# Two-layer spectral block on one core: the forward W transform folded on half rows (64x32 tiles), the inverse W transform in 64x64 tiles

## The chip, the cores and the metric

One of the eight cores of a Trainium2 chip runs the kernel. The metric is the device time of one execution in microseconds. Three executions of the kernel before gave 526.34 us as the median, 525.83 us as the lowest and 531.92 us as the highest.

## The reference

The input `x` has shape (4, 45, 90, 384): batch, H, W, channels. Two layers follow one another. Each takes a two-dimensional Fourier transform over H and W, keeps the 23 columns kw = 0 to 22 (all 45 rows of kh), mixes the channels in 8 blocks of 48 with two small dense layers, applies a soft threshold, transforms back and adds its input.

```
# layer 0                                       # layer 1
Xh = f.real - f.imag                            xr, xi = real(xs), imag(xs)
o1 = relu(Xk @ w1[0] + b1[0])                   o1r = relu(xr@w1[0] - xi@w1[1] + b1[0])
o2 = o1 @ w2[0] + b2[0]                         o1i = relu(xi@w1[0] + xr@w1[1] + b1[1])
spec = softshrink(o2, 0.01)                     o2r, o2i = softshrink(second dense layer)
y = ifft2(spec).real + x                        y = irfft2(o2r + 1j*o2i) + x
```

The kernel never goes back to the image between the layers. Layer 0's result is added in the frequency domain (only its even part along kh matters for kw = 0), and a single inverse transform at the end is added to `x` and written out.

## The kernel before

The work is split into 8 tasks, one per batch image and half of the channels (`HC` = 192). A task has six steps of four kw each (the last has three), so there are 48 steps (`STEPS`, `NSTEPS`). `schedule()` writes the order of all work by hand, and every engine walks through the same list, executes its own part and waits on semaphores. Each engine's queue is in order.

**Forward W** ("fwd", lines 402 to 408, 468 to 472, 552 to 574). An image lies in SBUF with W on 90 partitions (`img`, three buffers). A group is four rows of H. TensorE multiplies with `w_fwd` (90 of 128 rows, 64 columns) in two 128x64 tiles, each over 384 columns (two rows of H), into one PSUM bank of the pair P3. ScalarE (for task 0 VectorE, L472) copies the bank to `fs`, and SyncE writes it to DRAM scratch `scr_f` with two DMAs (L284). There are 12 groups per task, 23 DMAs. Groups of task t+1 run in steps 1, 2 and 3 of task t: two before A, two behind it.

**The step.** SyncE loads four kw of `scr_f` into `bt` (L297, 3,072 contiguous bytes per partition row). A is forward H (L618), copied by ScalarE and VectorE to `xs`; GpSimd computes re minus im (`xd`, L362). C0 and D0 (L634, L644, 64x64 tiles) are layer 0's dense layers. VectorE forms its soft-thresholded result `nt`, and GpSimd subtracts it from the real part in `xs` (L369). C1 and D1 (L656, L669) are layer 1's dense layers. T (L681) transposes `nt`, VectorE adds it to `ns` (L533), E (L694) is inverse H, copied to `et`, which SyncE writes to `scr_i` (L303).

**Inverse W** ("inv", L605 and L551). SyncE reads rows of `scr_i` into `jr` (L322, L326). A group is four rows of H: two 64x128 tiles, K = 48 of 64 rows, 90 of 128 columns, 384 moving columns each, into both banks of P3. VectorE adds both banks to `img` (90 x 768, L551); GpSimd stores eight rows (L378) and later loads the next image into their place (L354). In the last task the 12 groups use all eight banks, and four of them (`LAST_POOL`) are added by GpSimd behind a ScalarE copy (L456, L386).

The order within a step s is: load(s+2), C1(s-1), inverse, E(s-2), inverse, C0(s), D1(s-1), D0(s), two forward groups, A(s+1), two forward groups, T(s-1), inverse. Three inverse groups per step run in steps 3, 4, 5 and in step 0 of the task after.

```
for r in range(f_dmas(g)):
    a, b = h0 + 2 * r, min(h0 + 2 * r + 2, h1)
    last = mm(ps[64 * r:64 * r + 64, P3 + g % 2, 0:(b - a) * HC], K["w_fwd"],
              img[t % IMGS][:, a:b, :].rearrange("p h c -> p (h c)"), start=True, stop=True)
```

## Time and profile before

| what | us |
|---|---|
| median of three executions | 526.34 |
| the profiled execution, its own time | 527.67 |
| its span, first to last instruction | 525.8 |
| TensorE matmuls busy | 480.0 |
| VectorE busy | 303.9 |
| ScalarE busy | 208.8 |
| GpSimd busy | 172.8 |

The profile comes from one execution; 527.67 us lies 1.33 us above the median, and 1.9 us of it lie outside the span. PE is TensorE's matmuls, PEld its weight loads, DVE VectorE, ACT ScalarE, POOL GpSimd, SPq SyncE's queue of DMA issues. An fp32 matmul shows as two MATMUL records, so the number behind "x" in a row of PE is twice the number of matmuls in the code. In a timeline row the first number is the start, the second the time to the end of the last of the merged instructions; since matmuls overlap at their ends, the path is read from start to start.

### The profile page before, as it was taken

What the parts mean: (1) busy time and instruction counts of PE and PEld (TensorE: products, weight loads), DVE (VectorE), ACT (ScalarE), POOL (GpSimd) and SP (SyncE); (2) the same over time, 40 slices, a digit from 0 to 9 for tenths busy, and PEclk for the clock granted to TensorE, in tenths of its full rate; (3) what the DMA queues carried; (4) which work ended last, traced back from release to release, by engine and by line L of the source; (5) the groups of instructions that cost most, each with busy time, mean ns of one, the idle gap of its engine ahead of it and who ended that gap; (6) DMA issues with size and microseconds to landing.
All of it is one profiled execution on the core that took longest, in us unless ns stands there. A gap on an engine that the chain in (4) does not pass through costs nothing.

```text
span 525.8 us, 14875 instructions
## 1 busy us (share of the span) xinstructions
PE 480.0 (91%) x6144; PEld 347.5 (66%) x6144; DVE 303.9 (58%) x674; ACT 208.8 (40%) x473; POOL 172.8 (33%) x194
## 2 busy tenths in 40 slices
PE   4549999999999999999999999999999999998772
PEld 1137777767777677767777676777777777876531
DVE  6413456456764577456764577456763677566642
ACT  0014544554354433554354433454345433433101
POOL 9703133113432134313442133312442123222124
PEclk9858999999999999999999999999999999999967
DMA  8859955476899588877889688886989565735397
GB/s 187 268 141 218 272 149 150 105 205 181 253 222 244 154 210 246 238 202 184 263 216 236 173 208 242 228 213 176 255 221 248 167 175 156 156 84 141 108 242 223
DMA packets 76720, 104.65 MB, mean 199 GB/s; under 512 B 7761, under 2 KB 63303, under 8 KB 76526
## 3 DMA queue, kind: packets, MB, share of 16 engines
q1 hardware_dynamic: 57622, 55.97, 39.8%
q0 software_dynamic: 10608, 40.45, 29.1%
q10 hardware_dynamic: 8424, 7.28, 5.5%
q8 instruction: 50, 0.82, 0.7%
q14 instruction: 16, 0.13, 0.1%
HBM read 52.23 MB, written 51.43 MB: 197 GB/s over the span
## 4 chain that ended last, share of the span: by engine, by line
PE 79%; DMA 6%; DVE 6%; POOL 3%; ACT 2%; issue 2%; SPq 1%; ACTq 0%; POOLq 0%; DVEq 0%
PE ps L605 13%; PE ps L669 13%; PE ps L694 12%; PE ps L656 11%; PE ps L572 10%; PE ps L618 9%; PE ps L681 5%; PE ps L634 4%; DMA scr_f<-fs 3%; PE ps L644 3%; DVE img L551 2%; DVE ns L525 2%; ACT p L442 1%; POOL img L386 1%; POOL xs L369 1%
## 5 line engine op out<-in xcount | busy, mean ns | idle before, releaser
L551 DVE TENSOR_TENSOR img<-ps,img 90x768 f32<-90x768 f32 x92 | 82.7, 900 | 23.0 <-PE ps L605 18.1
L369 POOL TENSOR_TENSOR xs<-xs,nt 128x360 f32<-128x360 f32 (+1 forms) x48 | 41.5, 865 | 149.3 <-DVE nt L503 121.7
L605 PE MATMUL ps<-jr,cst 64*128 64x384 f32 (+1 forms) x358 | 83.6, 535 | 7.2 <-DVE img L551 5.7
L572 PE MATMUL ps<-img,cst 128*64 128x384 f32 (+1 forms) x368 | 72.2, 506 | 12.4 <-DMA img<-x 7.6
L378 POOL DMA_DIRECT2D y<-img x42 | 34.6, 825 | 136.0 <-DVE img L551 135.6
L618 PEld LDWEIGHTS ps<-cst,bt 128*64 128x64 f32 x1472 | 63.2, 141 | 21.0 <-issue 13.9
L435 ACT ACTIVATE o<-ps,wt 97x180 f32<-97x180 f32 (+1 forms) x96 | 33.8, 405 | 107.2 <-PE ps L656 107.1
L618 PE MATMUL ps<-cst,bt 128*64 128x90 f32 x1472 | 69.0, 248 | 6.7 <-DMA bt<-scr_f 6.7
L525 DVE SCALAR_TENSOR_TENSOR ns<-p,ps 109x384 f32<-109x384 f32 x96 | 53.2, 554 | 37.9 <-ACT p L442 33.0
L669 PE MATMUL ps<-wt,o 128*64 128x96 f32 x1472 | 73.9, 250 | 0.5 <-DVE o L517 0.5
L669 PEld LDWEIGHTS ps<-wt,o 128*64 128x64 f32 x1472 | 64.9, 137 | 12.6 <-issue 12.6
L656 PE MATMUL ps<-xs,wt 64*97 64x180 f32 (+1 forms) x768 | 68.6, 315 | 2.6 <-POOL xs L369 1.8
L694 PE MATMUL ps<-ns,cst 64*90 64x192 f32 x736 | 71.0, 323 | 0.0
L694 PEld LDWEIGHTS ps<-ns,cst 64*90 64x90 f32 x736 | 62.8, 155 | 7.4 <-issue 1.1
L656 PEld LDWEIGHTS ps<-xs,wt 64*97 64x97 f32 x768 | 57.4, 161 | 13.3 <-POOL xs L369 5.7
L442 ACT ACTIVATE p<-ps 109x384 f32<-109x384 f32 x96 | 47.0, 490 | 27.3 <-PE ps L669 27.3
L408 ACT ACTIVATE fs<-ps 112x384 f32<-112x384 f32 x84 | 38.9, 475 | 36.3 <-PE ps L572 27.2
L517 DVE TENSOR_SCALAR o<-ps,wt 97x180 f32<-97x180 f32 (+1 forms) x96 | 33.8, 394 | 33.3 <-PE ps L656 33.3
L572 PEld LDWEIGHTS ps<-img,cst 128*64 128x64 f32 x368 | 24.7, 141 | 40.7 <-issue 35.5
L488 DVE COPY xs<-ps 128x360 f32<-128x360 f32 (+1 forms) x48 | 24.8, 517 | 44.5 <-PE ps L618 44.5
L533 DVE TENSOR_TENSOR ns<-ps,ns 109x192 f32<-109x192 f32 x96 | 29.8, 352 | 33.5 <-PE ps L681 32.7
L605 PEld LDWEIGHTS ps<-jr,cst 64*128 64x128 f32 x358 | 32.1, 192 | 25.6 <-issue 13.0
(41 smaller groups left out, 411.5 us busy)
## 6 DMA issues: line engine op xcount, KB each, us to landing
y<-img POOLq DMA_DIRECT2D x35, 540.0 KB, 5.5
img<-x POOLq DMA_DIRECT2D x30, 540.0 KB, 8.5
scr_i<-et SPq DMA_DIRECT2D x48, 270.0 KB, 5.7
scr_f<-fs SPq DMA_DIRECT2D x176, 72.0 KB, 3.4
bt<-scr_f SPq DMA_DIRECT2D x40, 270.0 KB, 4.6
jr<-scr_i SPq DMA_DIRECT2D x48, 216.0 KB, 5.1
img<-x ACTq DMA_DIRECT2D x10, 540.0 KB, 7.4
y<-img SPq DMA_DIRECT2D x11, 270.0 KB, 3.8
```

The costliest lines, as they stand in the source:

```text
L369: nc.gpsimd.tensor_tensor(re, re, nt[s % 2][:, :, 0:kws(s), 0:H], ALU.subtract).then_inc(re_ok, 1)
L378: pool.dma_start(out[b, r0:r1, :, f * HC:(f + 1) * HC].rearrange("h w c -> w h c"), img[k][0:W, r0:r1, :]).then_inc(y_st[k][c], 16)
L408: nc.scalar.activation(fs[k][0:rows, 0:cols], ps[0:rows, P3 + g % 2, 0:cols], ACT.Copy).then_inc(f_cp, 1)
L442: nc.scalar.activation(p1[0:rows, p, :], ps[0:rows, P2 + p, 0:2 * HC], ACT.Relu).then_inc(d1_p, 1)
L525: nc.vector.scalar_tensor_tensor(out=ns[0:rows, p].rearrange("p n r c -> p (n r c)"), in0=p1[0:rows, p, :], scalar=2 * LAM, in1=ps[0:rows, ...
L551: nc.vector.tensor_tensor(y, p, y, ALU.add).then_inc(i_add, 1)
L572: last = mm(ps[64 * r:64 * r + 64, P3 + g % 2, 0:(b - a) * HC], K["w_fwd"], img[t % IMGS][:, a:b, :].rearrange("p h c -> p (h c)"), start= ...
L605: last = mm(ps[:, B0 + r, 0:n], K["w_inv"][64 * r:64 * r + 64, :], set_rows(t, j)[64 * r:64 * r + 64, at, 0:n], start=True, stop=True)
L618: last = mm(ps[64 * ab:64 * ab + 64, P0 + q, k * 2 * H:(k + 1) * 2 * H], bt[s % BT][:, at:at + 64], K["h_fwd"], start=True, stop=True)
L656: last = mm(ps[0:2 * BS + 1, P2 + ab, q * STEP * H:q * STEP * H + n], w1[k, im, 2 * f + q, :], xt[k, q, 0:kws(s), im * H:(im + 1) * H], st ...
L669: last = mm(ps[64 * r:64 * r + 64, P2 + p, b * 2 * BS:(b + 1) * 2 * BS], o11[:, b, 2 * p + r, :], w21[:, block_no(s // STEPS, b), :], star ...
L694: last = mm(ps[0:2 * H, P0 + r, p * HC:(p + 1) * HC], K[("h_inv_re", "h_inv_im")[im]][k, :], ns[k, p, :, im, :], start=im == 0, stop=im == 1)
```

## The change

Image rows are folded. W = 90 is cut into halves of 45 columns and H = 45 into halves of 23 and 22 rows: partitions 0 to 44 hold the W positions of the first H half, 64 to 108 those of the second, and the two W halves r = 0, 1 lie side by side in the free dimension. A group is now four j (rows of a half), that is eight rows of H; a task has six (`CH`).

- **New step "uv".** Before the forward matmuls VectorE writes u = half 0 + half 1 and GpSimd writes v = half 0 - half 1, each 128 x 768 fp32, both inputs in SBUF, into one of two buffers. u gives the even kw, v the odd ones.
- **Forward W.** Eight matmuls per group, K = 45 of 64 rows, 32 columns, 384 moving columns, in the eight 64x32 tiles of the array, into both banks of P3. ScalarE does both copies for all tasks. SyncE stores a group with eight DMAs of 24 partitions x 1,536 bytes: 48 per task.
- **Scratch layouts.** `scr_f` and `scr_i` have kw outermost and 48 slots of H instead of 45; a load into `bt` has 96 partition rows, each of four runs of 768 bytes.
- **Inverse W.** Still 12 groups per task; a group is now four j of both H halves for one W half: four 64x64 tiles of 384 columns. VectorE's addition has 109 partitions; the groups of the last set take two additions each.
- **Images.** Loads and stores are split by H half: 8 loads and 8 stores per task in four chunks, refills at their own places in the order. The buffers are cleared whole; `img1` is now cleared by VectorE and `img2` by GpSimd behind the forward groups of task 0. SyncE issues half of task 0's image loads.
- `FS` goes from 4 to 3, `JR` from 3 to 4, `LAST_POOL` from (1, 4, 7, 10) to (1, 4, 7, 9).

```diff
-IMGS, FS, BT, JR = 3, 4, 3, 3
-LAST_POOL = (1, 4, 7, 10)
-JSETS = [(0, 3), (3, 6), (6, 9), (9, 11), (11, 12)]
...
+WR, HR = W // 2, -(-H // 2)
+CH = -(-HR // 4)
+ROWS = 64 + WR
+GROUPS = 2 * CH
+CHUNKS = [(0, 2), (2, 4), (4, 5), (5, 6)]
+NXC = len(CHUNKS)
+IMGS, FS, BT, JR = 3, 3, 3, 4
+LAST_POOL = (1, 4, 7, 9)
+
+KWO = list(range(0, KWP, 2)) + list(range(1, KWP, 2))
+SLOTS = [(p, 4 * i + 2 * a + s) for a in range(2) for i in range(CH) for p in range(2) for s in range(2)]
...
+    order = [("uv", 0, 0), ("uv", 0, 1)]
+    for g in range(CH):
+        order.append(("fwd", 0, g))
+        if g + 2 < CH:
+            order.append(("uv", 0, g + 2))
+    order += [("clear", 1), ("clear", 2), ("load", 0), ("load", 1), ("a", 0), ("x", 0), ("x", 1)]
...
-            fwd[s] = [("fwd", t + 1, 4 * (i - 1) + k) for k in range(4)]
+            fwd[s] = [("fwd", t + 1, 2 * (i - 1) + k) for k in range(2)]
...
+        uv = [("uv",) + f[1:] for f in fwd[s]]
+        ahead = [("uv",) + f[1:] for f in fwd[s + 1]] if s + 1 < NSTEPS else []
...
+        order += uv[1:2]
...
-        order += fwd[s][0:2]
+            order.append(("x", 2 * s + 2))
+        order += fwd[s][0:1]
...
+        order += fwd[s][1:2]
...
+        order += ahead[0:1]
...
-        scr_f = [nc.dram_tensor(f"scr_f{t}", (H, 2, KWP, HC), F32, kind="Internal").ap() for t in range(TASKS)]
-        scr_i = [nc.dram_tensor(f"scr_i{t}", (KWP, 2, H, HC), F32, kind="Internal").ap() for t in range(TASKS)]
...
+        scr_f = [nc.dram_tensor(f"scr_f{t}", (KWP, 2, 2, CH, 2, 2, HC), F32, kind="Internal").ap() for t in range(TASKS)]
+        scr_i = [nc.dram_tensor(f"scr_i{t}", (KWP, 2, 2, 4 * CH, HC), F32, kind="Internal").ap() for t in range(TASKS)]
...
+        def x_loaded(t, g):
+            k, used, c = t % IMGS, t // IMGS, chunk_of(g)
+            if t == 0:
+                return x_first[g], 32
+            if t == 1:
+                return x_second[c], 32
+            return x_ld[k][c], 32 * (used + (k == 2))
...
+        def added(t, g):
+
+            before = [m for m in range(g + 1) if t < TASKS - 1 or m not in LAST_POOL]
+            return i_add, t * (GROUPS + 2) + len(before) + len([m for m in before if m // 2 == CH - 1])
...
+            for g in range(CH):
+                j0, j1 = jrange(g, g + 1, 1)
+                sp.wait_ge(x_odd if g % 2 else x_clr[0], g // 2 + 1)
+                sp.dma_start(folded(0, 1, j0, j1), rows_of(x[0], HR + j0, HR + j1, 0)).then_inc(x_first[g], 16)
...
-                    n, (h0, h1) = t * GROUPS + g, hrows(g)
+                    n = t * CH + g
                     k = n % FS
-                    sp.wait_ge(f_cp, n + 1)
-                    for r in range(f_dmas(g)):
-                        a, b = h0 + 2 * r, min(h0 + 2 * r + 2, h1)
-                        sp.dma_start(scr_f[t][a:b].rearrange("h e k c -> (e k) h c"),
-                                     fs[k][64 * r:64 * r + 2 * KWP, 0:(b - a) * HC].rearrange("q (h c) -> q h c", c=HC)).then_inc(f_st[k], 16)
+                    for p in range(2):
+                        sp.wait_ge(f_cp, 2 * n + p + 1)
+                        for a in range(2):
+                            for o in range(2):
+                                sp.dma_start(scr_f[t][o * KWP // 2:(o + 1) * KWP // 2, :, p, g, a].rearrange("k e s c -> (k e) (s c)"),
+                                             fs[k][64 * a + 32 * o:64 * a + 32 * o + KWP, p, :]).then_inc(f_st[k], 16)
...
-                    rows = scr_f[t].rearrange("h e k c -> (h e) k c")[:, STEP * i:STEP * i + kws(s), :]
-                    sp.dma_start(bt[s % BT][0:2 * H, 0:kws(s) * HC].rearrange("p (k c) -> p k c", c=HC), rows).then_inc(b_ld[s % BT], 16)
+                    rows = scr_f[t][STEP * i:STEP * i + kws(s)].rearrange("k e p g a s c -> (e p g a s) k c")
+                    sp.dma_start(bt[s % BT][0:2 * len(SLOTS), 0:kws(s) * HC].rearrange("p (k c) -> p k c", c=HC), rows).then_inc(b_ld[s % BT], 16)
...
+                        m = t * CH + j - JR
+                        sp.wait_ge(i_mm, 2 * (m + 1))
+                    for a in range(2):
+                        sp.dma_start(set_rows(t, j)[64 * a:64 * a + 2 * KWP].rearrange("q p c -> q (p c)"),
+                                     scr_i[t][:, :, a, 4 * j:4 * j + 4, :].rearrange("k e h c -> (k e) (h c)")).then_inc(landed, 16)
...
+                        c, p = divmod(s, 2)
+                        j0, j1 = jrange(*CHUNKS[c], p)
+                        pool.wait_ge(x_clr[2], 1)
+                        pool.dma_start(folded(2, p, j0, j1), rows_of(x[1], HR * p + j0, HR * p + j1, 0)).then_inc(x_ld[2][c], 16)
+                if kind == "clear" and what[0] == 2:
+                    nc.gpsimd.memset(img[2][:], 0.0).then_inc(x_clr[2], 1)
+                if kind == "uv":
                     t, g = what
-                    c, k, (b, f) = g // 2, t % IMGS, divmod(t, HALVES)
-                    r0, r1 = c * XCH, min(c * XCH + XCH, H)
-                    pool.wait_ge(i_add, t * GROUPS + g + 1)
-                    pool.dma_start(out[b, r0:r1, :, f * HC:(f + 1) * HC].rearrange("h w c -> w h c"), img[k][0:W, r0:r1, :]).then_inc(y_st[k][c], 16)
-                    if c > 0:
-                        refill(t, c - 1)
+                    n, (j0, j1) = t * CH + g, jrange(g, g + 1)
+                    pool.wait_ge(*x_loaded(t, g))
+                    if n >= 2:
+                        pool.wait_ge(f_mm, n - 1)
+                    nc.gpsimd.tensor_tensor(uv[n % 2][:, 1, 0:j1 - j0, :], img[t % IMGS][:, j0:j1, 0, :], img[t % IMGS][:, j0:j1, 1, :],
+                                            ALU.subtract).then_inc(v_ok, 1)
...
+                    t, g = what
+                    c, k, (b, f) = chunk_of(g // 2), t % IMGS, divmod(t, HALVES)
+                    pool.wait_ge(*added(t, g))
+                    for p in range(2):
+                        j0, j1 = jrange(*CHUNKS[c], p)
+                        pool.dma_start(rows_of(out[b], HR * p + j0, HR * p + j1, f), folded(k, p, j0, j1)).then_inc(y_st[k][c], 16)
+                if kind == "refill" and what[0] + IMGS < TASKS:
+                    t, c = what
+                    k, (b, f) = t % IMGS, divmod(t + IMGS, HALVES)
+                    pool.wait_ge(y_st[k][c], 32 * (t // IMGS + 1))
+                    for p in range(2):
+                        j0, j1 = jrange(*CHUNKS[c], p)
+                        pool.dma_start(folded(k, p, j0, j1), rows_of(x[b], HR * p + j0, HR * p + j1, f)).then_inc(x_ld[k][c], 16)
...
-                if kind == "fwd" and what[0] > 0:
+                if kind == "fwd":
...
-                    n, (h0, h1) = t * GROUPS + g, hrows(g)
-                    k, rows, cols = n % FS, (112, 2 * KWP)[g == GROUPS - 1], min(2, h1 - h0) * HC
+                    n = t * CH + g
                     if n >= FS:
-                        act.wait_ge(f_st[k], f_stored((n - FS) // GROUPS, (n - FS) % GROUPS))
...
-                    nc.scalar.activation(fs[k][0:rows, 0:cols], ps[0:rows, P3 + g % 2, 0:cols], ACT.Copy).then_inc(f_cp, 1)
+                    for p in range(2):
+                        nc.scalar.activation(fs[n % FS][:, p, :], ps[:, P3 + p, 0:2 * HC], ACT.Copy).then_inc(f_cp, 1)
...
-                if kind == "fwd" and what[0] == 0:
+                if kind == "clear" and what[0] == 1:
+                    nc.vector.memset(img[1][:], 0.0).then_inc(x_clr[1], 1)
+                if kind == "uv":
...
+                    if n >= 2:
+                        dve.wait_ge(f_mm, n - 1)
+                    nc.vector.tensor_tensor(uv[n % 2][:, 0, 0:j1 - j0, :], img[t % IMGS][:, j0:j1, 0, :], img[t % IMGS][:, j0:j1, 1, :],
+                                            ALU.add).then_inc(u_ok, 1)
...
-                    t, g = what
-                    h0, h1 = hrows(g)
...
+                    B0 = P3 if t < TASKS - 1 else 2 * (what[1] % 4)
+                    j0, j1 = jrange(g, g + 1)
+                    dve.wait_ge(i_mm, t * GROUPS + what[1] + 1)
+                    if j1 - j0 == 4:
+                        y = img[t % IMGS][0:ROWS, j0:j1, r, :].rearrange("p (a s) c -> p a s c", a=2)
+                        p = ps[0:ROWS, B0:B0 + 2, 0:2 * HC].rearrange("p a (s c) -> p a s c", s=2)
+                        nc.vector.tensor_tensor(y, p, y, ALU.add).then_inc(i_add, 1)
...
+                        for a in range(2):
+                            y = img[t % IMGS][0:ROWS, j0 + 2 * a:min(j0 + 2 * a + 2, j1), r, :]
+                            p = ps[0:ROWS, B0 + a, 0:(2, 1)[a] * HC].rearrange("p (s c) -> p s c", c=HC)
+                            nc.vector.tensor_tensor(y, p, y, ALU.add).then_inc(i_add, 1)
...
-                    for r in range(f_dmas(g)):
-                        a, b = h0 + 2 * r, min(h0 + 2 * r + 2, h1)
-                        last = mm(ps[64 * r:64 * r + 64, P3 + g % 2, 0:(b - a) * HC], K["w_fwd"],
-                                  img[t % IMGS][:, a:b, :].rearrange("p h c -> p (h c)"), start=True, stop=True)
+                    n = t * CH + g
+                    pe.wait_ge(u_ok, n + 1)
+                    pe.wait_ge(v_ok, n + 1)
+                    vacate(0)
+                    vacate(1)
+                    for a in range(2):
+                        for o in range(2):
+                            for p in range(2):
+                                q, m = 64 * p, 64 * a + 32 * o
+                                last = mm(ps[m:m + 32, P3 + p, 0:2 * HC], w_fwd[q:q + 64, o, :],
+                                          uv[n % 2][q:q + 64, o, 2 * a:2 * a + 2, :].rearrange("w s c -> w (s c)"), start=True, stop=True)
                     last.then_inc(f_mm, 1)
-                    tenant[g % 2] = [(f_cp, t * GROUPS + g + 1)]
+                    for p in range(2):
+                        tenant[p] = [(f_cp, 2 * n + p + 1)]
...
-                    for r in range((h1 - h0 + 1) // 2):
-                        n = min(2, h1 - h0 - 2 * r) * HC
-                        last = mm(ps[:, B0 + r, 0:n], K["w_inv"][64 * r:64 * r + 64, :], set_rows(t, j)[64 * r:64 * r + 64, at, 0:n], start=True, stop=True)
+                            pe.wait_ge(*last_added(what[1] - 4))
+                    for p in range(2):
+                        for a in range(2):
+                            m, c = (min(2, HR - 4 * g - 2 * a)) * HC, slice(64 * a, 64 * a + 64)
+                            last = mm(ps[64 * p:64 * p + 64, B0 + a, 0:m], w_inv[c, r, :], set_rows(t, g)[c, p, 0:m], start=True, stop=True)
                     last.then_inc(i_mm, 1)
-                    tenant[0] = tenant[1] = [(i_add, t * GROUPS + g + 1)]
```

## Rows read from the trace of the kernel before

**Rows 1.** The page's first two parts: busy time by engine, span in 40 slices.
```profile
PE 480.0 (91%) x6144; PEld 347.5 (66%) x6144; DVE 303.9 (58%) x674; ACT 208.8 (40%) x473; POOL 172.8 (33%) x194
...
PE   4549999999999999999999999999999999998772
...
PEclk9858999999999999999999999999999999999967
```

**Rows 2.** The page's chain that ended last, by engine.
```profile
PE 79%; DMA 6%; DVE 6%; POOL 3%; ACT 2%; issue 2%; SPq 1%; ACTq 0%; POOLq 0%; DVEq 0%
```

**Rows 3.** TensorE's timeline, steps without inverse: start us, duration us, what.
```profile
207.38 1.46 PE L618 MATMUL ps<-cst,bt 128*64 128x90 f32 x32
208.88 0.66 PE L681 MATMUL ps<-cst,nt 128*109 128x128 f32 x4
...
215.18 1.51 PE L572 MATMUL ps<-img,cst 128*64 128x384 f32 x8
216.52 1.41 PE L618 MATMUL ps<-cst,bt 128*64 128x90 f32 x32
217.76 1.46 PE L572 MATMUL ps<-img,cst 128*64 128x384 f32 x8
219.15 0.69 PE L681 MATMUL ps<-cst,nt 128*109 128x128 f32 x4
...
221.09 1.46 PE L694 MATMUL ps<-ns,cst 64*90 64x192 f32 x16
222.48 0.54 PE L634 MATMUL ps<-xd,wt 64*64 64x180 f32 x8
```

**Rows 4.** The same timeline, a step with inverse groups.
```profile
230.80 0.81 PE L605 MATMUL ps<-jr,cst 64*128 64x384 f32 x4
231.44 1.47 PE L694 MATMUL ps<-ns,cst 64*90 64x192 f32 x16
232.75 0.92 PE L605 MATMUL ps<-jr,cst 64*128 64x384 f32 x4
233.60 0.54 PE L634 MATMUL ps<-xd,wt 64*64 64x180 f32 x8
234.07 1.54 PE L669 MATMUL ps<-wt,o 128*64 128x96 f32 x32
235.54 0.54 PE L644 MATMUL ps<-o,wt 64*64 64x180 f32 x8
```

**Rows 5.** All engines' timeline of the start: GpSimd's clears, SyncE's stores of task 0.
```profile
9.02 14.65 POOL L344 MEMSET img<- 64x8640 f32 x2
...
9.86 16.63 SPq L284 DMA_DIRECT2D scr_f<-fs  x23
```

**Rows 6.** The chain of waits at the start: the first A.
```profile
31.16 2.69 PE ps L618 x32
```

**Rows 7.** SyncE's queue in steady state, two steps with forward groups.
```profile
222.26 1.98 SPq L284 DMA_DIRECT2D scr_f<-fs  x4
...
226.38 4.72 SPq L284 DMA_DIRECT2D scr_f<-fs  x8
```

**Rows 8.** Groups of instructions, shapes apart: busy us, mean ns, idle before.
```profile
L551 DVE TENSOR_TENSOR img<-ps,img 90x768 f32<-90x768 f32 x84 | 79.9, 953 | 21.7 <-PE ps L605 16.9
...
L408 ACT ACTIVATE fs<-ps 112x384 f32<-112x384 f32 x77 | 37.5, 490 | 36.3 <-PE ps L572 27.2 <-DMA scr_f<-fs 9.0
...
L386 POOL TENSOR_TENSOR img<-p,img 90x768 f32<-90x768 f32 x4 | 7.3, 1818 | 5.8 <-ACT p L456 5.8
```

**Rows 9.** DMA issues: count, KB each, median us to landing.
```profile
scr_i<-et SPq DMA_DIRECT2D x48, 270.0 KB, 5.7
...
bt<-scr_f SPq DMA_DIRECT2D x40, 270.0 KB, 4.6
```

**Rows 10.** VectorE's timeline in the step of rows 4.
```profile
233.87 0.94 DVE L551 TENSOR_TENSOR img<-ps,img 90x768 f32<-90x768 f32 x1
234.73 0.39 DVE L492 TENSOR_SCALAR o<-ps,wt 128x180 f32<-128x180 f32 x1
```

More of the change, by code:

```diff
@@ L103, in schedule @@
 def schedule():
-    order = [("fwd", 0, g) for g in range(GROUPS)]
-    order += [("load", 0), ("load", 1), ("a", 0), ("x", 0)]
+    order = [("uv", 0, 0), ("uv", 0, 1)]
[4 more added lines that the diff above has]
+    order += [("clear", 1), ("clear", 2), ("load", 0), ("load", 1), ("a", 0), ("x", 0), ("x", 1)]
     fwd, inv = [[] for _ in range(NSTEPS + 2)], [[] for _ in range(NSTEPS + 2)]
@@ L141, in schedule @@
             order += [("rows", t - 1, j) for j in range(JR)]
-        order += fwd[s][2:4]
-        if s < 2:
-            order.append(("x", 2 * s + 2))
+        if i == 1 and t > 1:
+            order.append(("refill", t - 2, 2))
+        order += fwd[s][1:2]
+        if s < 3:
+            order.append(("x", 2 * s + 3))
         if 0 < s <= NSTEPS:
@@ L147, in schedule @@
         order += inv[s][2:3]
+        order += ahead[0:1]
+        if i == 1 and t > 1:
+            order.append(("refill", t - 2, 3))
     order += held
-    order += [("rows", TASKS - 1, j) for j in range(len(JSETS))]
+    order += [("rows", TASKS - 1, j) for j in range(CH)]
     order += [("inv", TASKS - 1, g) for g in range(GROUPS)]
@@ L265, in last_added @@
                 return i_pool, LAST_POOL.index(g) + 1
-            return i_add, (TASKS - 1) * GROUPS + len([m for m in range(g + 1) if m not in LAST_POOL])
+            return added(TASKS - 1, g)
         def block_no(t, n):
@@ new lines, in _ @@
+                if kind == "inv" and what[0] < TASKS - 1 and (what[1] + 1) // 2 in [b for a, b in CHUNKS] and what[1] % 2 == 1:
+                    t, g = what
[4 more added lines that the diff above has]
+                        pool.dma_start(rows_of(out[b], HR * p + j0, HR * p + j1, f), folded(k, p, j0, j1)).then_inc(y_st[k][c], 16)
```

229 lines of the change are left out of this document (96 added, 133 removed).

## The prediction

> **What bounds the kernel now.** I read the page's busy times first: TensorE's matmuls take 480.0 of 525.8 us, no other engine more than 304, and from the fourth slice to the thirty-sixth TensorE is at 9 tenths or more [rows 1]. The chain that ended last says the same by another road: 79% of it is TensorE, SyncE's issues 1%, DMA 6% [rows 2]. So between about 40 and 475 us time is TensorE's start-to-start time, step by step, and I take it from its timeline. The start and the tail are different: in the first three slices TensorE is at 4 to 5 tenths, and the first A begins at 31.16 us [rows 6]. There the order is loads, forward W, stores, load, A, and nothing covers it. A change that makes TensorE cheaper and the road to the first A longer gains in one place and loses in the other.
>
> **Forward W on TensorE, -15.7 us.** Today a step with forward groups spends 1.34 us on the first two groups, 1.24 on A between them, 1.39 on the other two: 3.97 us [rows 3]. An inverse group is two waves of 384 columns in two tiles and takes 0.64 us to the next start [rows 4]: 0.32 us a wave. C0, two waves of 180 columns in four tiles, takes 0.47 us [rows 4]; at 0.15 a wave that leaves 0.17 for changing tile shape on both sides. A takes 1.50 us between operations of other shapes and 1.24 between forward groups of its own shape [rows 3]. The new group is 16 records in eight tiles: two waves if all eight run side by side, so 2 x 0.32 + 0.17 = 0.81 us. Then the step costs 0.81 + 1.50 + 0.81 = 3.12, 0.85 less. 21 steps (7 tasks) give 17.9; today's 12th group streams a quarter of the others' columns, which I count as 0.3 us a task, 2.2 in all, so 15.7. No row shows four column tiles. The bound above is that only four tiles run at once, as in C0: four waves, 1.45 us a group, 4.40 a step, which is 0.43 x 21 + 2.2 = 11.2 us more than today. I take eight, because the four of C0 did run as four. The Trainium skill, "TensorEngine Tiling (Array Packing)", section "Available Configurations", lists 64x32 as eight independent tiles; that would be the same 0.81.
>
> **Inverse W on TensorE, +7 us.** The waves don't change: two waves of 384. What changes is the neighbour. The first group of a step now sits between C1 and E, all in 64-row, 128-column tiles, and costs 0.64 [rows 4]. In 64x64 tiles it costs 0.81, and C1 and E each pay part of a change, 0.06 to 0.1 (E takes 1.39 before C0 without an inverse group between and 1.31 before one [rows 3, 4]): +0.3. The second, between E and C0 (0.85 today), now has C0's shape: -0.15. The third, behind T, pays again before C1: +0.1. Net +0.25 for three; 26 such sets of three give +7. Ends: 0 if the drain hides, +12 if each change costs the 0.17 in full and more.
>
> **The start, +12 us.** SyncE issues 23 stores from 9.86 us in 16.63 us, the last at about 26.5, and A starts 4.7 us later [rows 5, 6]. It will issue 48. GpSimd has done its first clears at 9.02 us [rows 5]; v takes 1.8 (as 90 x 768 in L386), the first group 1.5 (0.81 at a clock that falls as low as 5 tenths in the first three slices [rows 1]), ScalarE's two copies 1.0 [rows 8], so the first store leaves at 13.5. In steady state SyncE issues one per 0.50 us (4 in 1.98) to 0.59 (8 in 4.72) [rows 7]. I take 0.50: 24 us, last store at 37.5, 11 later than now. `bt` loads are cut from 3,072-byte to 768-byte runs, like `scr_i`'s stores of the same size, 5.7 us against 4.6 [rows 9]: +1.1. A starts at 43.3. Low end: if small DMAs went out as fast as v and u allow (6 x (1.8 + 0.95) = 16.6 us), +5; high end 0.59 each, +16. The clears of `img1` (VectorE) and `img2` (GpSimd) take 7.3 us each if both go like GpSimd's two in 14.65 [rows 5]. They lie beside the stores; without that cover they would add up to 7.
>
> **VectorE and ScalarE in the steps, +7 us.** u costs 0.95 us if it goes like the inverse addition of the same 768 elements [rows 8]; one is queued between E's copy and the second inverse addition. In a step with inverse groups today the addition runs from 233.87 to 234.81 and C0's relu from 234.73 to 235.12; D0, which needs it, starts at 235.54 [rows 4, 10]. 0.95 more makes the relu end at 236.1; with about 0.1 us that TensorE itself is later by then, D0 waits about 0.4; the 109-partition addition and the other u, behind T, I put at another 0.4. Such steps: 6, so 5 us. In the 15 steps without inverse the relu has 0.8 us less to do and the wait is near nothing. ScalarE makes two copies of 0.49 [rows 8] behind one group; behind T the third inverse group needs both banks, T lasts 0.6 and the copies 1.1: 0.4 x 6, 2 us. GpSimd's 48 v's, 1.8 us each, come to 87 us, and split image DMAs to about 20 more; it is busy 172.8 of 525.8 us [rows 1] and the v's are queued behind `xd`, whose next customer is half a step off, so I cost them at nothing. If that cover fails C1 waits for L369 up to 1.8 us a step.
>
> **SyncE in steps 1 to 3, +2 us.** There it issues 48 stores, 8 loads into `jr` in step 1, 2 in step 3, and 6 others: 64 x 0.50 = 32 us between the first forward group and the last, for about 24 us of step time. The backlog of some 8 us must be gone before the load for the next task, which waits for the last stores. That load then lands (32 + 1.3 + 3 + 5.7) about 42 us after the first group; the A that needs it comes about 42 us after it too (4.4 steps of some 9.6). I take 0.3 us a task; at 0.59 an issue it is 6 us a task, 40 in all. In a step without forward groups the queue drains.
>
> **The tail, +1 us:** two more store issues; the four GpSimd additions stay as they are.
>
> **Sum.** 12 - 15.7 + 7 + 7 + 2 + 1 = +13.3 on the profiled execution's 527.67 us: 541.0. The median lies 1.3 below it: 539.7; I say 540.
>
> **Rivals.**
> 1. *Covers hold, slower becomes not slower* (chance 0.28). Its place is SyncE's queue at the start: if a store of 24 rows is issued in 0.35 us rather than 0.50, v and u set the pace and the first A is only 5 us later; no backlog either. With the inverse at +3 and the steps' waits at 1, the sum is 5 - 15.7 + 3 + 1 + 1 = -6, so 520 as a median. It decides below about 0.37 us an issue. For it: isolated issues; against it: the unbroken stretch of four at 0.50 [rows 7].
> 2. *Four tiles at a time* (0.12). 27 us on top of the forecast, less about 5 of waits that the longer groups cover: 562. Nothing in the rows speaks for it but the lack of a row.
> 3. *u and v exclude each other* (0.15). Both read two operands in SBUF; no row shows VectorE and GpSimd doing that together. If u must wait for v, it ends up to 1.8 us later; in the 6 full steps that comes on top of a full VectorE queue (+0.9 x 6), in the other 15 half of it reaches D0 (+0.3 x 15), so +10: 550. The Trainium skill, "SBUF — State Buffer", section "Who interferes with whom", states that a VectorE instruction with two SBUF inputs and a GpSimd instruction that reads SBUF exclude one another for the whole instruction. No row of this case tests that rule.
>
> The forecast itself has 0.45, with its own range 531 to 548.
>
> **How the numbers follow.** About 2% (10.5 us, to 536.9 or 515.8) is what a measurement of this kernel tells from no change. Faster: only the lower part of rival 1, 0.11. Within 2%: the rest of rival 1, 0.17, the part of the forecast below 537, 0.13, and a little of rival 3, 0.05: 0.35. Slower: the rest of these and rival 2, 0.54. The range reaches from rival 1's centre less 2 to rival 2's near side, 518 to 556; about 0.1 lies below it and 0.1 above.
>
> **What would show it.** The first A at 41 to 45 us, with SyncE issuing without a break before it; a forward group of 16 records 0.8 us to the next start (1.45 is rival 2); an inverse group between C1 and E 0.8; D0 waiting for L492's relu in steps with inverse groups; u's mean near 0.95 us (above 1.4 is rival 3); A waiting for `bt` at a task's end if SyncE's backlog is worse. A median under 530 would mean that SyncE's issue time was wrong.

## The result: 13% slower, and outside the predicted range

The changed kernel takes 599.15 us (median of four, 597.23 to 600.24) against 526.92 us beside it; the ratio is 1.1346, interval 1.1265 to 1.1427. The direction was as forecast, the size was not: 540 was said, 556 was the upper end. The profiled execution spans 596.2 us, that of before 525.8. Ratios below leave out executions more than 1.5% above their kernel's fastest (three of four in e1, one of four in e4 and in b1).

The page after, its counterparts in [rows 1, 2]:

```profile
span 596.2 us, 16944 instructions
...
PE 480.8 (81%) x6944; PEld 329.9 (55%) x6944; DVE 365.5 (61%) x728; ACT 210.0 (35%) x485; POOL 274.3 (46%) x267
...
PE   1417779989989987989989985899869997998653
...
PEclk9999899999999999999979996899979999999967
...
PE 34%; DMA 31%; SPq 14%; DVE 8%; POOL 5%; issue 4%; ACT 2%; ACTq 0%; DVEq 0%; POOLq 0%
DMA bt<-scr_f 13%; SPq L325 10%; DMA img<-x 10%; PE ps L665 6%; DMA scr_f<-fs 6%; PE ps L716 6%; PE ps L652 5%; PE ps L741 5%; PE ps L703 4%; PE ps L622 4%; DVE uv L515 4%; DMA jr<-scr_i 2%; PE ps L728 2%; PE ps L691 2%; SPq L361 1%
```

TensorE is busy as long as before, but the chain is no longer TensorE's: its 79% are 34%, and SyncE's store issues (L325), the load of `bt`, the stores to `scr_f` and the image loads hold 39%. Slices of 5 to 8 stand in TensorE's row where there was an unbroken 9, and the granted clock falls in the same places (7, 6 and 8, 7), which it never did in the middle before.

The groups that changed most (busy us, mean ns of one, idle before them) and the DMA issues, for [rows 8, 9]:

```profile
L409 POOL TENSOR_TENSOR uv<-img 128x768 f32<-128x768 f32 (+1 forms) x48 | 99.3, 2081 | 25.7 <-DMA img<-x 25.3
L665 PE MATMUL ps<-cst,bt 128*64 128x90 f32 x1472 | 73.6, 257 | 32.8 <-DMA bt<-scr_f 32.8
...
L515 DVE TENSOR_TENSOR uv<-img 128x768 f32<-128x768 f32 (+1 forms) x48 | 63.9, 1331 | 27.8 <-DMA img<-x 25.6
...
bt<-scr_f SPq DMA_DIRECT2D x40, 288.0 KB, 6.7
```

A (L665) now waits 32.8 us for `bt` (6.7 before); u (L515) and v (L409) wait 25 us each for image loads, and with them everything behind them on VectorE and GpSimd. u takes 1331 ns, not 950.

I split each profiled span at the first and the last A:

| kernel | first A | first to last A | last A to the end |
|---|---|---|---|
| before | 31.2 | 444.2 | 50.4 |
| changed | 40.0 | 499.3 | 56.9 |
| difference | +8.8 | +55.1 | +6.5 |

The forecast had +12 for the start, +0.3 for the steps (-15.7 + 7 + 7 + 2) and +1 for the tail. So the steps are what has to be explained.

**What TensorE itself does is as forecast.** Its timeline after, for [rows 3, 4] (start us, duration us):

```profile
251.24 0.88 PE L622 MATMUL ps<-uv,cst 64*32 64x384 f32 x16
252.04 1.46 PE L665 MATMUL ps<-cst,bt 128*64 128x90 f32 x32
253.44 0.88 PE L622 MATMUL ps<-uv,cst 64*32 64x384 f32 x16
254.24 0.69 PE L728 MATMUL ps<-cst,nt 128*109 128x128 f32 x4
...
256.27 0.88 PE L652 MATMUL ps<-jr,cst 64*64 64x384 f32 x8
257.08 1.54 PE L741 MATMUL ps<-ns,cst 64*96 64x192 f32 x16
...
263.00 0.54 PE L691 MATMUL ps<-o,wt 64*64 64x180 f32 x8 [1.08 <-DVE o L536]
...
267.73 0.88 PE L652 MATMUL ps<-jr,cst 64*64 64x384 f32 x8 [0.56 <-ACT fs L450]
```

A group of 16 records takes 0.80 us to the next start: eight tiles run side by side. A between two groups takes 1.40. The inverse group between C1 and E takes 0.81. The bracket says how long the engine stood before a row and for what: D0 1.08 us for VectorE's relu, the inverse group behind T 0.56 us for ScalarE's copy. Behind the relu's lateness stands a load, for u came late itself:

```profile
260.92 0.76 DVE L515 TENSOR_TENSOR uv<-img 128x576 f32<-128x576 f32 x1 [1.33 <-DMA img<-x]
```

**What the steps lose.** The step lengths show it by kind; step k runs from one A to the next, and ends at the A that takes load k. Where that is the first or second load of a new task, which SyncE issues behind that task's last stores, the step takes 11 to 17 us rather than 9.2 to 9.9 (k = 18, 30, 31, 36, 37, 42, 43), 22 us in all. The step in which u and v first want a new image takes 10.6 to 14.9 rather than 9.1 (k = 14, 20, 26, 32, 38), 23 us in all; one of these, k = 20, ends on a wait for `bt` as well. Another 8 us are in k = 2 to 4, behind the first images. The chain of waits into the longest one, k = 31 (start us, us, what; above, a store issue every 0.41 us):

```profile
337.91 2.69 SPq L325
...
340.64 1.55 SPq L325
...
342.23 5.50 DMA scr_f<-fs
...
347.86 19.63 DMA bt<-scr_f x2
...
367.62 1.43 PE ps L665 x15
```

The "x2" is two loads, one behind the other, with an A between them (TensorE's timeline from 350 to 352 us):

```profile
351.01 1.19 PE L665 MATMUL ps<-cst,bt 128*64 128x90 f32 x25 [1.62 <-DMA bt<-scr_f]
```

And SyncE's queue behind it, for [rows 7]:

```profile
350.21 1.87 SPq L338 DMA_DIRECT2D bt<-scr_f  x1
352.17 3.76 SPq L344 DMA_DIRECT2D scr_i<-et  x1
355.97 2.37 SPq L338 DMA_DIRECT2D bt<-scr_f  x1
...
359.95 5.17 SPq L338 DMA_DIRECT2D bt<-scr_f  x1
```

The last store's issue begins at 342.23, the store lands 5.5 us later, and only then, at 347.86, does the first load for the next task go out. That one lands in 3.0 us; A waited 1.6 for it. The load that the A at 367.62 waits for is the second, issued at 350.21: it takes 17.3 us to land, in a stretch in which the 16 DMA engines are 93% busy (second row: us, busy us by engine, clock, DMA share, GB/s):

```profile
338.00:348.00 10.00, 9.77 (x148) 6.89 (x146) 7.58 (x15) 3.84 (x9) 2.04 (x3) 1.00 0.59 131
348.00:367.00 19.00, 10.84 (x166) 7.67 (x160) 9.33 (x25) 4.64 (x11) 8.29 (x11) 0.91 0.93 252
```

A single issue now holds SyncE for 1.9 to 5.2 us, where [rows 7] had 0.5 to 0.6. The load into k = 20 is the extreme: issued at 221.66, no later ahead of its A than before (21.5 us, 20.3 before), it landed only after 21.4 us.

```profile
221.66 21.38 DMA bt<-scr_f
...
243.18 1.48 PE ps L665 x32
```

### The profile page after: what moved, and what is told of

Same layout as the page of the kernel before. It is cut to its first block, busy times and chain, and to the rows that moved or that the text cites. A ratio compares the mean times of both kernels' runs of the same rounds, so it can differ in the third digit from the quotient of the medians.

```text
span 596.2 us, 16944 instructions
## 1 busy us (share of the span) xinstructions
PE 480.8 (81%) x6944; PEld 329.9 (55%) x6944; DVE 365.5 (61%) x728; ACT 210.0 (35%) x485; POOL 274.3 (46%) x267
## 4 chain that ended last, share of the span: by engine, by line
PE 34%; DMA 31%; SPq 14%; DVE 8%; POOL 5%; issue 4%; ACT 2%; ACTq 0%; DVEq 0%; POOLq 0%
DMA bt<-scr_f 13%; SPq L325 10%; DMA img<-x 10%; PE ps L665 6%; DMA scr_f<-fs 6%; PE ps L716 6%; PE ps L652 5%; PE ps L741 5%; PE ps L703 4%; PE ps L622 4%; DVE uv L515 4%; DMA jr<-scr_i 2%; PE ps L728 2%; PE ps L691 2%; SPq L361 1%
## 5 line engine op out<-in xcount | busy, mean ns | idle before, releaser
L409 POOL TENSOR_TENSOR uv<-img 128x768 f32<-128x768 f32 (+1 forms) x48 | 99.3, 2081 | 25.7 <-DMA img<-x 25.3
L665 PE MATMUL ps<-cst,bt 128*64 128x90 f32 x1472 | 73.6, 257 | 32.8 <-DMA bt<-scr_f 32.8
L652 PE MATMUL ps<-jr,cst 64*64 64x384 f32 (+1 forms) x736 | 82.6, 511 | 18.4 <-DVE img L593 7.4
L665 PEld LDWEIGHTS ps<-cst,bt 128*64 128x64 f32 x1472 | 64.9, 147 | 55.2 <-issue 42.8
L593 DVE TENSOR_TENSOR img<-ps,img 109x768 f32<-109x768 f32 x76 | 72.5, 956 | 26.8 <-PE ps L652 25.3
L716 PE MATMUL ps<-wt,o 128*64 128x96 f32 x1472 | 77.8, 257 | 11.4 <-DVE o L561 11.3
L515 DVE TENSOR_TENSOR uv<-img 128x768 f32<-128x768 f32 (+1 forms) x48 | 63.9, 1331 | 27.8 <-DMA img<-x 25.6
L741 PE MATMUL ps<-ns,cst 64*96 64x192 f32 x736 | 73.2, 330 | 0.0
L741 PEld LDWEIGHTS ps<-ns,cst 64*96 64x96 f32 x736 | 60.7, 161 | 17.0 <-issue 16.1
L703 PEld LDWEIGHTS ps<-xs,wt 64*97 64x97 f32 x768 | 56.1, 162 | 20.7 <-issue 10.1
L622 PE MATMUL ps<-uv,cst 64*32 64x384 f32 x768 | 47.3, 553 | 19.7 <-POOL uv L409 13.8
L388 POOL TENSOR_TENSOR xd<-xs 128x360 f32<-128x360 f32 (+1 forms) x48 | 38.3, 798 | 45.0 <-DVE xs L532 44.5
L450 ACT ACTIVATE fs<-ps 128x384 f32<-128x384 f32 x96 | 41.9, 488 | 47.8 <-PE ps L622 43.5
L490 ACT ACTIVATE et<-ps 96x384 f32<-96x384 f32 x48 | 23.4, 487 | 68.9 <-PE ps L741 56.1
```

The costliest lines, as they stand in the source:

```text
L409: nc.gpsimd.tensor_tensor(uv[n % 2][:, 1, 0:j1 - j0, :], img[t % IMGS][:, j0:j1, 0, :], img[t % IMGS][:, j0:j1, 1, :], ALU.subtract).then_ ...
L515: nc.vector.tensor_tensor(uv[n % 2][:, 0, 0:j1 - j0, :], img[t % IMGS][:, j0:j1, 0, :], img[t % IMGS][:, j0:j1, 1, :], ALU.add).then_inc(u ...
L593: nc.vector.tensor_tensor(y, p, y, ALU.add).then_inc(i_add, 1)
L622: last = mm(ps[m:m + 32, P3 + p, 0:2 * HC], w_fwd[q:q + 64, o, :], uv[n % 2][q:q + 64, o, 2 * a:2 * a + 2, :].rearrange("w s c -> w (s c)" ...
L652: last = mm(ps[64 * p:64 * p + 64, B0 + a, 0:m], w_inv[c, r, :], set_rows(t, g)[c, p, 0:m], start=True, stop=True)
L665: last = mm(ps[64 * ab:64 * ab + 64, P0 + q, k * 2 * H:(k + 1) * 2 * H], bt[s % BT][:, at:at + 64], K["h_fwd"], start=True, stop=True)
```

## The experiments

The changed kernel's two new waits were the two theories: A, that u and v at the head of in-order queues wait for image loads; B, that SyncE's stores delay `bt`. Rival 3 of the prediction stood beside them.

**e1_prev_image**: u and v read the image of the task before, so that they wait for no load (GpSimd's line; VectorE's is changed alike).

```diff
-                    pool.wait_ge(*x_loaded(t, g))
+                    pool.wait_ge(*x_loaded(max(t - 1, 0), g))
```


> The changed kernel, but u and v of task t are formed from the image of task t-1, so they never wait for a load (the output differs; the last task's additions take over the wait for its image). All instructions and transfers stay. Theory A (the additions u and v stand ahead of the steps' work in VectorE's and GpSimd's in-order queues and wait there for an image that is loaded later than before): the steps that lost 10.2+14.1+12.1 and 5 to 6 us at every task's second step become normal, about 27 us less than the changed kernel's 599, so 572. Theory B (SyncE's twice as many stores): image loads are not its concern, under 5 us, 595 or more.

Measured 601.15 us (580.98 to 609.95). These times spread too far to say what the edit is worth alone; e3 asks it again. The profiled execution (608.38) does show that the edit did what it was meant to: u waits 6.1 us for images in all, not 25.6, and v 0.5, not 25.3. But A still waits 34.6 us for `bt`, and k = 19, 25, 31 and 37, the second load of four tasks, take 16 to 18 us.

**e2_four_stores**: a group is stored with four DMAs of 64 partitions instead of eight of 24; the bytes rise by a third, the count halves (the scratch layout and the counts of the waits follow, not shown).

```diff
-                            for o in range(2):
-                                sp.dma_start(scr_f[t][o * KWP // 2:(o + 1) * KWP // 2, :, p, g, a].rearrange("k e s c -> (k e) (s c)"),
-                                             fs[k][64 * a + 32 * o:64 * a + 32 * o + KWP, p, :]).then_inc(f_st[k], 16)
+                            sp.dma_start(scr_f[t][:, :, p, g, a].rearrange("k e s c -> (k e) (s c)"),
+                                         fs[k][64 * a:64 * a + 64, p, :]).then_inc(f_st[k], 16)
```


> The changed kernel with four store DMAs per forward group instead of eight (64 partitions each, the padding rows written too, a third more bytes); everything else unchanged, output unchanged. Theory B (SyncE's issue of 384 stores delays the first A and the load at each task's end): first A at 33 to 35 us instead of 40.0, the waits of A for bt at the task ends (2.1, 1.9, 6.7, 2.2, 4.7, 1.7, 2.4 us) gone: about 27 us less, 572. Theory A alone: only the start moves, 6 us, 593. Theory C (the loads of bt land late because their runs are 768 bytes, not because they are issued late): the start moves by 5, the waits at the task ends stay.

Measured 570.27 us (566.27 to 573.52), ratio 1.0843 (1.0782 to 1.0903): 29 us less, as theory B said, although more bytes are written. Steps k = 18, 30, 31, 36, 37, 42 and 43 are all 9.4 us again. From first to last A it is 471.4 us, 28 less (in the fastest of the four executions); the first A comes at 36.9, 3.1 sooner and not the 5 to 7 expected. A's wait for `bt` is little more than a quarter of what it was:

```profile
L665 PE MATMUL ps<-cst,bt 128*64 128x90 f32 x1472 | 71.6, 252 | 9.9 <-DMA bt<-scr_f 8.9
```

The loads still have 768-byte runs, so theory C, that these alone make them late, is out. Landings of 16 to 17 us are still there (k = 15, 21, 27, 33, 39), but these loads are issued 21 to 25 us ahead of their A and nothing waits. What is shown is that fewer, larger stores cure the waits; the count alone is not, because the shape changed with it. A store of 64 rows takes 0.60 us to issue (median) where one of 24 took 0.37, so that a group's issues fell only from 2.95 to 2.39 us.

**e5_two_stores**: two DMAs a group, each with both banks; the scratch layout of e2.


> The changed kernel with two store DMAs per forward group instead of eight, so 12 per task. Against the one with four (570): if SyncE still bounds anything, another 5 to 10 us less; if four were enough, 568 to 572, with the waits for the image loads at every task's second step (3 to 5 us each) left.

Measured 568.36 us (565.46 to 573.36), ratio 1.0824. Halving once more gives 2 us, inside both kernels' spread. With four stores SyncE was no longer late at any step's end.

**e3_both**: e1's edit on e2.


> Both edits together (u and v from the previous image, four stores per group). If the two causes are separate and together explain the loss: 599 - 27 - 27 = 545, and the rest against 527 is the start, the tail and the waits of the steps with both kinds of groups. If they share one cause (loads late because the transfer engines are full), the sum is well short of the two gains: 560.

Measured 554.94 us (553.75 to 557.79), ratio 1.0563 (1.0522 to 1.0603): 15 us less than e2. The steps k = 14, 26, 32, 38 fall from 12.9 to 13.6 us to about 10. The loads' wait is real and about half the size of what e2 took away. 555 lies between the two expectations, 545 and 560: the two causes are separate, but the second is worth 15 us and not 27.

**e4_no_v**: e3, with v cut to two elements a row, so that VectorE's u has the data to itself.


> As the one with both edits, and GpSimd's v leaves out all but two elements per partition (v stays zero, the output differs). Theory of the shared port (u waits for v and v for u): u's mean falls from 1.33 to 0.95 us, GpSimd loses 96 us of busy time, D0's and D1's waits for VectorE shrink: 6 to 10 us less than with v. If VectorE and GpSimd do not disturb each other, u stays at 1.33 us and the time moves by less than 2 us, but for the start, where v paces the groups.

Measured 548.61 us (547.02 to 553.29, the fourth execution 558.99), ratio 1.0419 (1.0375 to 1.0463): 6 us less than e3 by the medians, 8 by the ratios, with 6 to 10 expected. u's mean falls from 1366 to 923 ns, and none of the 48 is over 1.13 us. In e3 20 were over 1.14.

**b1_double_stores**: the kernel before, with 46 stores a task for its 23.

```diff
+                        for e in range(2):
+                            sp.dma_start(scr_f[t][a:b, e].rearrange("h k c -> k h c"),
```


> The kernel before the change with each of its forward store DMAs cut in two (real and imaginary rows apart): 46 stores per task instead of 23, the same bytes and runs, nothing else changed. Theory B (the number of SyncE's issues is what costs): 23 more issues of 0.41 us put the first A at about 40 us instead of 31.2, and in steps 1 to 3 of each task SyncE falls behind as in the changed kernel, so A waits for bt at the task ends: +9 and +15, 550. Rival (the stores cost only at the start; in the steps something of the changed kernel's own, its u and v or its image loads, makes the rest): +9, 535.

Measured 545.20 us (541.36 to 547.25, the fourth execution 552.96), ratio 1.0362 (1.0307 to 1.0417). Twice as many stores of the same bytes, each of 23 rows for 46, cost the old kernel 19 us, without folding, u, v or another tile shape. The profile is that of the slowest execution, 552.96. Its first A is at 35.9 us, 4.7 later (9 expected); SyncE's row at the start reads

```profile
9.87 21.67 SPq L285 DMA_DIRECT2D scr_f<-fs  x46
```

which is 0.47 us an issue. The rest of the 19 is in the steps and the tail. There it is only in part the wait expected: between 60 and 490 us one A waits for `bt`, 6.0 us at k = 24. Otherwise ScalarE's copies wait for stores to land before they may write a buffer again, 20.9 us (9.0 before), and the inverse groups stand behind the copies for 7.1 us (0.8 before):

```profile
L409 ACT ACTIVATE fs<-ps 112x384 f32<-112x384 f32 x77 | 37.8, 491 | 45.8 <-PE ps L573 24.9 <-DMA scr_f<-fs 20.9
```

**b2_inv64**: the kernel before, with its inverse W in four 64x64 tiles a group.

```diff
+                        for q in range(2):
+                            last = mm(ps[64 * q:64 * q + 64, B0 + r, 0:n], K["w_inv"][64 * r:64 * r + 64, 64 * q:64 * q + 64], set_rows(t, j)[64 * r:64 * r + 64, at, 0:n], start=True, stop=True)
```


> The kernel before the change with each inverse matmul of a 64x128 tile done as two of 64x64 tiles: the same waves of 384 columns, the tile shape of the changed kernel, the same output. The prediction's term: the changes of tile shape beside C1 and E cost 0.25 us for three groups, +7 us, 533. Rival: the drains hide or weigh double, 527 or 541.

Measured 529.75 us (529.22 to 530.31), ratio 1.0079 (1.006 to 1.0099): +4.0 us for the inverse's new shape. The forecast had +7.

**e6_fine_chunks**: e5, with six image chunks instead of four, refilled as early as each is free.

```diff
-CHUNKS = [(0, 2), (2, 4), (4, 5), (5, 6)]
+CHUNKS = [(g, g + 1) for g in range(CH)]
```


> The one with two stores per group, and images stored and loaded in six chunks of one group instead of four, each refill moved up by up to a step and a half (output unchanged, 24 loads and 24 stores... that is 12 and 12 per task instead of 8 and 8). Theory A (what is left in the steps is the wait of u and v for late loads): like the kernel whose u and v take the previous image, 555 or a little less. If more and smaller image transfers only shift the lateness: 565 or more.

Measured 566.32 us (565.77 to 568.08), ratio 1.0771: 2 us, where I expected 13. The waits for the image went (u's from 24.7 to 8.6 us in all), and k = 14, 26, 32, 38 are at 10.0 to 10.2 (11.1 to 13.6 in e5); but the next step in three tasks, k = 27, 33, 39, takes 15.3, 14.6 and 14.5 us, against 13.0, 12.3 and 8.9 in e5 and 8.9 each in e2. VectorE's and GpSimd's timelines there:

```profile
297.91 5.09 DVE L518 TENSOR_TENSOR uv<-img 128x768 f32<-128x768 f32 x1
302.93 0.71 DVE L564 TENSOR_SCALAR o<-ps,wt 97x180 f32<-97x180 f32 x2
```

```profile
297.31 1.28 POOL L427 DMA_DIRECT2D img<-x  x2
298.61 3.57 POOL L412 TENSOR_TENSOR uv<-img 128x768 f32<-128x768 f32 x2
```

u, an operation of 0.95 us when alone (e7 below), started at 297.91 and ended at 303.00, 0.8 us after the second v. D1's relu (L564) stands behind u. (u had 1.5 us beside no v, more than it needs, so it was not simply halted for the time of the two; what it lost when the first v began, the profile doesn't show.)

**e7_u_first**: e6, with v of a group behind its u.

```diff
+                    pool.wait_ge(u_ok, n + 1)
                     nc.gpsimd.tensor_tensor(uv[n % 2][:, 1, 0:j1 - j0, :], img[t % IMGS][:, j0:j1, 0, :], img[t % IMGS][:, j0:j1, 1, :],
```


> e6_fine_chunks with one wait more: GpSimd begins the subtraction v of a group only when VectorE has written u of the same group. In e6 u took 5.1 us at 297.9, 364.4 and 429.9 us, and v was running or queued twice in a row beside it (v v: 3.57 us from 298.61); D1 behind it stood 3.3 us, and five steps took 14 to 15 us instead of 9. Theory (an addition of VectorE with two SBUF inputs and a GpSimd subtraction cannot run side by side, and the one that comes second waits the other out): u now runs alone, takes 0.95 us nearly always (mean under 1.05; mean 1.66 in e6), those steps fall to 10 to 11 us, and the time to about 555, though v now holds GpSimd a little longer. Rival (u is long because of the DMAs that write the image and read the scratch at that time, not because of v): u stays at 3 to 5 us there, time 566 or more. Second rival (v behind u delays xd, re and GpSimd's refills by more than u gains): u's mean falls to 0.95 but the time stays at 562 to 572.

Measured 554.73 us (552.93 to 554.99), ratio 1.0528 (1.049 to 1.0567): the 555 of the theory, 11.6 us less for an added wait. k = 27, 33, 39 are 8.9 to 9.9, and u's mean is 1101 ns (1662 in e6, under 1050 expected). The same place of VectorE's and GpSimd's timelines:

```profile
300.34 0.95 DVE L519 TENSOR_TENSOR uv<-img 128x768 f32<-128x768 f32 x1
```

```profile
299.71 1.28 POOL L428 DMA_DIRECT2D img<-x  x2
301.46 1.81 POOL L413 TENSOR_TENSOR uv<-img 128x768 f32<-128x768 f32 x1 [0.47 <-DVE uv L519]
```

u ran at its own 0.95 beside GpSimd's image DMA issue (299.71 to 300.99), which stood beside the long u of e6 too: so it is v, not the issues, that held u. The first A, however, went from 37.0 to 43.5 us; from first to last A the kernel is 20.7 us shorter. The added wait keeps v behind the u of its own group only: the u of the next group can still fall beside it, and takes about 1.5 us when it does.

**e8_more_fs**: e7, with the wait only from task 1 on and `FS` = 6.


> e7_u_first with two edits in task 0's start: GpSimd's v waits for u only from task 1 on (in e7 the first A was at 43.5 us, in e6 at 37.0), and six buffers between the forward copies and their stores instead of three (in b3 eight instead of four brought the first A from 31.2 to 28.0 us). Theory (v and u take turns anyway at the start, and the wait only puts them in the worse order; the buffers take away stalls of TensorE of 1 to 3 us): first A at 34 to 36 us, time 546. Rival (24 stores from each of v and u's pace set the start, buffers are not short): first A at 37, time 548. If the order of v and u is worth nothing and something else made e7's start late: first A above 40 and 552 or more.

Measured 542.81 us (541.75 to 544.49), ratio 1.033 (1.0293 to 1.0367); 546 was expected. First A at 33.7 us: 9.8 sooner than e7, 3.3 sooner than e6. It is the fastest of the folded kernels, 56 us under the changed one, and still 3% behind the kernel before. The order and the buffers at the start changed together here.

**b3_more_fs**: the kernel before with `FS` = 8.

```diff
-IMGS, FS, BT, JR = 3, 4, 3, 3
+IMGS, FS, BT, JR = 3, 8, 3, 3
```


> The kernel before with eight buffers between the forward copies and their stores instead of four (FS = 8); nothing else. In the kernel before TensorE stands 3.87 us at 17.8 us for a buffer whose stores have not landed, and the chain holds 7.88 us of landing there. If the landing of stores sets the start, the first A comes 2 to 4 us sooner than 31.2 and the time is 522 to 524 (ratio 0.993 to 0.996). If SyncE's 23 issues in 16.6 us set it, the first A stays within 1 us of 31.2 and the time within 0.2% of 526. In the steps either says no difference.

Measured 521.84 us (519.99 to 523.04), ratio 0.9906 (0.9872 to 0.994): 0.9% faster than the kernel before, clear of noise though within the 2% counted as no change. In the chain the last load leaves at 24.83 and A starts at 28.02:

```profile
24.83 3.14 DMA bt<-scr_f
...
28.02 2.69 PE ps L618 x32
```

From first to last A it takes 443.1 us (444.2 before): of the 4.7 us between the two profiled spans, 3.1 are in the start.

## Why the prediction was wrong

**The start (+12; measured +8.8).** First store at 13.67 us (13.5 said), 48 issues in 21.42 us, 0.446 each rather than 0.50, A 4.9 us behind the last:

```profile
13.67 21.42 SPq L325 DMA_DIRECT2D scr_f<-fs  x48
36.40 1.36 SPq L338 DMA_DIRECT2D bt<-scr_f  x3
```

Rival 1, which needed 0.37, is out. That SyncE's count sets the first A is two fifths true: e5 issues 12 stores and its first A still comes at 36.5. Part of the rest is too few buffers, for e8, with six buffers and e6's order at the start, gains 3.3 us on e6. That v's and u's pace makes the remaining 2.5 over before is not shown: e4, with next to no v but two more clears ahead, starts at 37.4 like e3.

**Forward W (-15.7; right in mechanism, -18.2 in size).** 0.80 + 1.40 + 0.80 = 3.00 us a step against 3.97: 0.97 x 21 = 20.4, less the 2.2 of the short group, is 18.2. TensorE's busy time agrees: b2 and e8 differ by the fold and what came with it, and have 484.5 and 469.4 us. Rival 2 (four tiles, 1.45 us a group) is refuted.

**Inverse W (+7; +4.0 by b2).** The sign and the mechanism hold; the groups take 0.81 before E and 0.69 before C0 (272.23 to 272.92), as worked out. The small parts came out otherwise, though nearly in balance: in b2 E takes 1.47 us before the second group (1.31 to 1.34 before) and C1 1.42 (1.33), but C0 takes 0.42, not 0.47, and the group behind T 0.08 more, for the 0.1 said.

**VectorE and ScalarE (+7; the sum right, half of it by luck).** ScalarE's wait is there as named, 0.56 us where I said 0.4 to 0.5. In e8, with everything else repaired, the inverse groups wait 4.0 us between 60 and 490 us, for 2 said. D0's wait is not what I described. The 1.08 us above had an image load behind it. In e8's step with both kinds of groups D0 waits 0.1 us (at 242.12), not 0.4; the 0.4s stand in the step of the first forward groups (281.35, 341.7 and 402.0), where u takes 1.53 us beside v. All D0 waits in e8 come to 7.0 us, 2.84 of them once, at 70.3, where the first images load: 8 us in all without that one, against 7. "GpSimd's v costs nothing" was wrong: the forward groups stand 6.6 us there, in four tasks 0.77 and 0.88 us in one step, until v is done:

```profile
282.66 0.88 PE L627 MATMUL ps<-uv,cst 64*32 64x384 f32 x16 [0.77 <-issue]
...
285.81 0.88 PE L627 MATMUL ps<-uv,cst 64*32 64x384 f32 x16 [0.88 <-issue]
```

```profile
279.95 2.60 POOL L414 TENSOR_TENSOR uv<-img 128x768 f32<-128x768 f32 x1
...
283.88 1.83 POOL L414 TENSOR_TENSOR uv<-img 128x768 f32<-128x768 f32 x1
```

The v's end at 282.55 and 285.71, the groups start 0.1 us later. So the fold gains nothing even in e8: the four tasks from k = 14 to k = 38 take 240.9 us there and took 237.7 before, 0.8 more each. TensorE has less to do and waits longer.

**SyncE in steps 1 to 3 (+2): this is the step that failed.** It was mis-sized by more than 20 us: e2's edit to the stores takes 28 us out of the steps in the profiled executions, about 25 at the medians, and A's waits for `bt` fall by 23. b1's doubled stores put some 14 into the kernel before, in part by another path, the buffers. Two things in the term were wrong. I priced the mean issue, 0.50 us, and counted a backlog of 8 us that just drains. The queue kept 0.446 over 48 issues at the start, but in the steps the 62 issues from 308.90 to 344.81 took 35.9 us, 0.58 each, because single ones took far longer than the mean: three took 6.90 us at 337.91, one `bt` load 5.17 at 359.95. So the first load of a task went out late. And I gave the load 5.7 us to land, from the median of 4.6 [rows 9] and the shorter runs. The first did so, in 3.0; the second, issued later than it should have been and beside the image traffic, took 17.3, and the third of another task 21.4. My own text had 6 us a task at 0.59 an issue, as the far end of that term; it belonged in the range, which stopped at 556.

**A term was missing: the image loads.** I cost "split image DMAs" as GpSimd's time, never as a wait. Before, forward matmuls waited for the image, and they come late in a step; now u is first in VectorE's queue and v in GpSimd's, half a step ahead. 15 us by e3. A part of a `y` chunk must be added and stored before its place is loaded; with chunks of four inverse groups that is late.

**Rival 3 (u and v exclude each other; +10, chance 0.15) did happen**, besides the rest and not in its place. e7 against e6 is 11.6 us, e4 against e3 6 to 8. That is the rule cited in the prediction from the Trainium skill, "SBUF — State Buffer", section "Who interferes with whom", and the traces agree that the two stand in each other's way. On who goes first they don't agree: the page gives the whole instruction to the one that starts first, and in e6 u began 0.7 us before the first v and ended 0.8 us behind the second. I priced it as one v (1.8 us) that u waits for; beside two queued v's u lasted 4.1 us longer.

**The tail (+1; +6.5).** I counted two store issues. The chain shows the first row of the last sets: the DMA behind the issue at 563.24 takes 11.40 us, and TensorE stands until 575.04.

```profile
560.69 2.53 DMA scr_i<-et
...
563.24 0.31 SPq L361
...
563.60 11.40 DMA jr<-scr_i
...
575.04 1.54 PE ps L652 x5
```

No run took this apart; that the `y` stores beside it slow it is only argued. With the finer image chunks of e6 to e8 the tail is 52.6 to 54.0 us rather than 56.1 and 56.5 in e2 and e5, so about half of the +6.5 goes with the large chunks.

**The clock multiplied the waits.** The changed kernel's 6,944 matmul records took 480.8 us, the same records in e8 469.4: 11.4 us more, because after the long waits TensorE ran at 1.2 GHz for stretches of up to 10 us (the 6 and 7 in the row of the granted clock). No term of the sum had that.

By steps from the changed kernel down: four stores -29, two -2, finer and earlier image chunks -2, u ahead of v -12, buffers and order at the start -12: 599 to 543. What e8's profiled span has over that of before, 14.3 us, is 2.5 in the start, 8.2 from first to last A and 3.6 in the tail. In the middle part stand the inverse shape (+4, b2), the first image loads (k = 4 takes 12.8 us, 9.7 before), and the waits for v and the relu that eat the fold's 15 to 18 us.

**Still open:** why one load takes 17 to 21 us to land when another of its kind takes 3 to 5 (the DMA engines' share of 0.93 is beside it, no run changed it alone); whether it is the stores' number or their shape that counts, since both changed in e2 (24 rows to 64) and in b1 (46 to 23); and how e1's edit would stand alone.

## What to carry to other kernels

Before saving matmuls, count the DMAs of one queue between two of its deadlines: cutting the stores in two cost 19 us in a kernel that did nothing else differently. What stands behind them goes out late, and what waits for their buffers waits longer. Then ask how far ahead of its use each load is issued, and compare that with the longest landing in the trace, not with the median. An elementwise step that is put ahead of a matmul inherits the matmul's waits and puts them at the head of an in-order queue; ask what stands behind it there. Where VectorE and GpSimd read the same kind of data together, the order between them is worth writing down: a wait more made the kernel 12 us faster.

## What was unexpected in the hardware

- A `bt` load of 288 KB landed 3.5 us after its issue at the start, 6.7 as the median, and 21.4 at the most (issued 221.66, landed 243.04).
- One DMA issue on SyncE, 0.37 us as the median of the changed kernel, took up to 5.17 us.
- An addition of 128 x 768 on VectorE with both inputs in SBUF, 0.95 us alone, took 5.09 us beside two GpSimd subtractions of 1.8 us that were queued back to back; it did not get in between them.
- Eight fp32 tiles of 64x32, 384 columns each, ran as one: 16 records in 0.80 us from start to start, no longer than eight records in four 64x64 tiles (0.81).
- Four more buffers in front of the stores made the kernel before 0.9% faster, mostly in the start, although a small store at the head of the chain took as long to land as before (7.97 us in b3, 7.88 without them).
- Doubling the stores of the kernel before made ScalarE's copies wait 20.9 us for a free buffer, not 9.0.
